# A four-layer cross-attention stack: the two batches in flight are moved half a pipeline apart, and the large cross attention is cut in three

## What is computed

```python
# per batch (8 of them): x is 256 x 128, ctx is 512 x 96, all fp32
h = x + attn(ln(x), ln(x), 16 heads of 64)          # layer 0: the large one
h = h + attn(ln(h), ctx, 16 heads of 64)            #   (its scores have 512 keys)
h = h + (lin * gelu_tanh(gate)) @ w_ff2             #   gated feed-forward, 512 wide
h = ln(softmax(ln(h W_text) . ln(ctx W_audio)) (ctx W_audio) W_out + h)   # layer 1: one head
h = ln(h); h = h + attn(h, h, 16 heads of 8)        # layer 2: self attention
h = h + attn(ln(h), ctx, 16 heads of 8)             #   cross attention
h = h + gelu(ln(h) W1) W2                           #   feed-forward
h = h + attn(rotary, l2-normalised, keys and values from ctx, 16 heads of 8)  # layer 3
```

## Time and profile before

| what | value |
|---|---|
| median of 3 runs | 2421.76 us |
| the profiled execution's own time | 2438.8 us |
| its span | 2436.9 us |
| TensorE busy | 1946.3 us (80%) |
| TensorE weight load busy | 1506.8 us (62%) |
| VectorE busy | 1490.8 us (61%) |
| ScalarE busy | 1381.5 us (57%) |
| GpSimd busy | 228.8 us (9%) |
| granted TensorE clock, mean | 0.91 |
| DMA | under 1% but for the first slice |

### The profile page before, as it was taken

One profiled execution on the slowest core, in us unless ns is written; L12 is line 12 of the kernel. 1 busy time (PEld: TensorE's weight loads), 2 busy tenths in 40 slices (PEclk: granted clock), 3 DMA queues, 4 the chain that ended last, 5 costly groups with the idle time before them and its releaser, 6 DMA issues. The chain is left out here.

```text
span 2436.9 us, 40770 instructions
## 1 busy us (share of the span) xinstructions
PE 1946.3 (80%) x13984; PEld 1506.8 (62%) x13984; DVE 1490.8 (61%) x3423; ACT 1381.5 (57%) x3690; POOL 228.8 (9%) x488
## 2 busy tenths in 40 slices
PE   1889886777789987777778998777778898867877
PEld 1777665655577765555557776555556776656654
DVE  2667557775267665677436756567644665667763
ACT  1556555766455654576645554556665555446765
POOL 0000012111100001111100000121020000011111
PEclk7999998998899998898879999889888999989998
DMA  6000000000000000000000000000000000000000
GB/s 127 6 1 1 1 1 1 1 1 1 17 1 1 1 1 1 1 1 1 1 17 1 1 1 1 1 1 1 1 8 9 1 1 1 1 1 1 1 1 5
DMA packets 24162, 13.78 MB, mean 6 GB/s; under 512 B 9264, under 2 KB 23472, under 8 KB 23952
## 3 DMA queue, kind: packets, MB, share of 16 engines
q1 hardware_dynamic: 23952, 11.05, 2.0%
HBM read 9.99 MB, written 1.05 MB: 5 GB/s over the span
## 5 line engine op out<-in xcount | busy, mean ns | idle before, releaser
L1000 ACT ACTIVATE probs<-scores,nmax 128x512 f32<-128x512 f32 (+1 forms) x1024 | 586.6, 579 | 171.4 <-DVE nmax L1407 169.7
L1407 DVE TENSOR_REDUCE nmax<-scores 128x1 f32<-128x512 f32 (+1 forms) x768 | 519.6, 684 | 127.2 <-PE scores L403 73.5
L471 PE MATMUL turned<-ident,probs 128*128 128x128 f32 x3072 | 502.8, 289 | 73.2 <-ACT probs L1000 71.1
L471 PEld LDWEIGHTS turned<-ident,probs 128*128 128x128 f32 x3072 | 383.4, 148 | 164.5 <-ACT probs L1000 119.0
L773 PE MATMUL heads_out<-probs_t,v 128*32 128x256 f32 (+1 forms) x4096 | 389.0, 421 | 8.8 <-issue 4.3
L829 ACT ACTIVATE probs_t<-turned 128x512 f32<-128x512 f32 x384 | 229.1, 597 | 102.6 <-PE turned L471 96.3
L1420 DVE COPY probs_t<-turned 128x512 f32<-128x512 f32 x384 | 261.7, 681 | 26.5 <-PE turned L471 26.1
L773 PEld LDWEIGHTS heads_out<-probs_t,v 128*32 128x32 f32 (+1 forms) x4096 | 187.8, 129 | 139.3 <-issue 58.0
L740 PE MATMUL scores<-k_t,q_mask 128*128 128x256 f32 (+1 forms) x512 | 195.3, 430 | 75.4 <-POOL q_mask L1535 37.0
L1432 DVE TENSOR_TENSOR out_t<-heads_out,scale_t 128x256 f32<-128x256 f32 x192 | 81.5, 425 | 272.2 <-ACT scale_t L829 272.2
L1535 POOL CAST q_mask<-q_t 32x256 fp32r<-32x256 f32 x384 | 156.2, 407 | 659.4 <-PE scores L740 222.9
(11 more groups left out here) (309 smaller groups left out, 3273.3 us busy)
## 6 DMA issues: line engine op xcount, KB each, us to landing
out_t<-ctx_dram SPq DMA_DIRECT2D x8, 192.0 KB, 2.6
v<-wqt_dram SPq DMA_DIRECT2D x2, 512.0 KB, 5.1
wo<-wo_dram SPq DMA_DIRECT2D x2, 512.0 KB, 6.4
x<-x_dram SPq DMA_DIRECT2D x8, 128.0 KB, 2.4
y_dram<-x SPq DMA_DIRECT2D x8, 128.0 KB, 1.8
v<-wkt_dram SPq DMA_DIRECT2D x1, 512.0 KB, 5.0
probs_t<-wv_dram SPq DMA_DIRECT2D x1, 512.0 KB, 6.6
wff<-wff_dram SPq DMA_DIRECT2D x1, 512.0 KB, 5.8
```

Source lines behind the costliest of these rows:

```text
L471: return nc.tensor.transpose(out, in_, ident[:, :])
L1000: last = nc.scalar.activation(probs[:, n % 3, k * S:k * S + ph.keys], bank[:, k * S:k * S + ph.keys], ACT.Exp, bias=nmax[:, h * QB + qb:h ...
L1407: nc.vector.tensor_reduce(out, src, AX.X, ALU.max, negate=True).then_inc(sem["attention_max"], 1)
```

## The change

The two streams run half a pipeline apart: while stream a is in layer 0 (self0 and cross0), stream b is in layers 2 and 3. cross0 is cut in three phases of 6, 6 and 4 heads (12, 12 and 8 units), and the phases of the two streams alternate. Per half round there are seven phases: self0 of a beside mid1 of b; self2 of b beside mid0 of a; cross0a beside mid2 of b; cross2 of b with no chain; cross0b beside mid3 of b; l3 of b with no chain; cross0c beside the end of b and the start of its next batch. The first segment now holds a lone start, self0, mid0 and cross0 of batch 0 (with the start of batch 1), and the last one ends with a drain: mid1, self2, mid2, cross2, mid3, l3 and end of the last batch, each alone.

The bank X is needed by layer 0 in most phases now, so the chains use it as a second bank only in mid0 and in the drain; mid2 and mid3, which had it before, have Y alone in the loop. `v1` gets its own buffer, `scale_t` has one slot in place of two, and the loads are issued between the stores.

```diff
-PAIR = [("self0", 0, [("start", 1)]), ("self0", 1, [("mid0", 0)]), ("cross0", 0, [("mid0", 1)]),
-        ("cross0", 1, [("mid1", 0)]), ("self2", 0, [("mid1", 1)]), ("self2", 1, [("mid2", 0)]),
-        ("cross2", 0, [("mid2", 1)]), ("cross2", 1, [("mid3", 0)]), ("l3", 0, [("mid3", 1)])]
+def half_round(a, b, start=True):
+
+    return [("self0", a, [("mid1", b)]), ("self2", b, [("mid0", a)]), ("cross0a", a, [("mid2", b)]),
+            ("cross2", b, []), ("cross0b", a, [("mid3", b)]), ("l3", b, []),
+            ("cross0c", a, [("end", b)] + ([("start", b)] if start else []))]
+
+
+def drain(s):
+
+    return [("", 0, [("mid1", s)]), ("self2", s, []), ("", 0, [("mid2", s)]), ("cross2", s, []),
+            ("", 0, [("mid3", s)]), ("l3", s, []), ("", 0, [("end", s)])]
 
 
 SEGMENTS = {
-    "first": [("", 0, [("start", 0)])],
-    "loop": PAIR + [("l3", 1, [("end", 0), ("start", 0)]), ("", 0, [("end", 1)])],
-    "last": PAIR + [("l3", 1, [("end", 0)]), ("", 0, [("end", 1)])],
+    "first": [("", 0, [("start", 0)]), ("self0", 0, []), ("", 0, [("mid0", 0)]),
+              ("cross0a", 0, [("start", 1)]), ("cross0b", 0, []), ("cross0c", 0, [])],
+    "loop": half_round(1, 0) + half_round(0, 1),
+    "last": half_round(1, 0, start=False) + drain(1),
 }
...
-    spare = content in ("g1", "l1", "s1", "p1", "qkv1", "up1", "kv1", "qt1", "kt1", "kt3", "t1")
-    if chain == "start":
-        spare = s == 0 and content in ("v1", "v3")
-    return "spare" if spare and (chain, s) != ("mid1", 0) else "chain"
+    if chain == "mid0":
+        spare = content in ("v1", "v3", "v5", "v7")
+    else:
+        alone = SEGMENT == ["last"] and s == 1 and chain != "start"
+        spare = alone and content in ("g1", "l1", "s1", "p1", "qkv1", "up1", "kv1", "qt1", "kt1", "kt3", "t1")
+    return "spare" if spare else "chain"
...
 PACE = {
-    ("mid0", 0): {"hat": 0.5, "v2": 4, "v4": 1.6, "v5": 1.6, "v7": 4},
...
-    ("start", 1): {"ctx": 0.8, "stats": 4, "ln1": 0.64, "split": 6.25, "v0": 1.6, "v1": 4, "v3": 2.5},
+    "mid0": {"hat": 0.5, "v2": 4, "v4": 1.6, "v5": 1.6, "v7": 4},
+    "mid1": {"l0": 0.3},
+    "mid3": {"unit": 1.6},
+    "end": {"wo": 4},
+    "start": {"ctx": 0.8, "ln1": 0.64, "split": 4, "v0": 1.6, "v1": 1.6, "v3": 2.5},
 }
...
-        scale_t = sb("scale_t", [P, 2, S])
+        scale_t = sb("scale_t", [P, S])
...
             with sp.Fori(0, LOOPS) as b:
                 enter("loop")
-                load(1, b * STREAMS + 1)
-                store(0, b * STREAMS)
-                load(0, b * STREAMS + 2)
-                store(1, b * STREAMS + 1)
+                for s in range(STREAMS):
+                    store(s, b * STREAMS + s)
+                    load_context(s, b * STREAMS + s + 2)
+                    stored(s)
+                    load_tokens(s, b * STREAMS + s + 2)
                 segment_over()
```

More of the change, by code:

```diff
@@ L84 @@
 MAKE = {"self0": lambda s: Attention("self0", s, 2, S, t_rows=D),
-        "cross0": lambda s: Attention("cross0", s, 2, T, t_rows=C),
+        "cross0a": lambda s: Attention("cross0a", s, 2, T, t_rows=C, heads=(0, 6)),
+        "cross0b": lambda s: Attention("cross0b", s, 2, T, t_rows=C, heads=(6, 12)),
+        "cross0c": lambda s: Attention("cross0c", s, 2, T, t_rows=C, heads=(12, H)),
         "self2": lambda s: Attention("self2", s, 4, S, masked=True),
@@ L138 @@
             "pads": "mid1", "squares": "mid3", "root": "mid3"}
+SEGMENT = []
 ORDER = []
@@ L166, in enter @@
 def enter(segment):
-    for table in (ORDER, PHASES, FILL, NORM, SPLIT):
+    for table in (SEGMENT, ORDER, PHASES, FILL, NORM, SPLIT):
         table.clear()
+    SEGMENT.append(segment)
     fills = {"chain": 0, "spare": 0}
@@ L195, in precedes, with groups_out @@
     return first in ORDER and ORDER.index(first) < ORDER.index(second)
+def groups_out(layer, s, chain, group):
+    for (name, ps), ph in PHASES.items():
+        at = group - ph.first // ph.group
+        if name.startswith(layer) and ps == s and 0 <= at < ph.groups and precedes((name, s), (chain, s)):
+            return ph.at("out_scaled", at + 1)
+    return 0
 def early_t(ph):
@@ L211 @@
 PACE = {
-    ("mid0", 0): {"hat": 0.5, "v2": 4, "v4": 1.6, "v5": 1.6, "v7": 4},
-    ("mid0", 1): {"hat": 0.25, "astats": 0.6, "v1": 1.6, "audio_t": 0.6, "v4": 1.6, "v5": 1.6, "v7": 8},
-    ("mid1", 0): {"l0": 0.3},
-    ("mid1", 1): {"that": 0.4, "text_t": 0.4, "p1": 0.4, "qkv1": 2.5, "qt1": 0.5, "kt0": 0.5},
-    ("mid2", 1): {"stats": 0.3},
-    ("mid3", 0): {"unit": 1.6},
-    ("mid3", 1): {"unit": 1.6},
-    ("start", 1): {"ctx": 0.8, "stats": 4, "ln1": 0.64, "split": 6.25, "v0": 1.6, "v1": 4, "v3": 2.5},
+    "mid0": {"hat": 0.5, "v2": 4, "v4": 1.6, "v5": 1.6, "v7": 4},
[3 more added lines that the diff above has]
+    "start": {"ctx": 0.8, "ln1": 0.64, "split": 4, "v0": 1.6, "v1": 1.6, "v3": 2.5},
 }
 def due(steps, units):
-    pace = [PACE.get((name, s), {}).get(step, 1.0) for name, s, step in steps]
+    pace = [PACE.get(name, {}).get(step, 1.0) for name, s, step in steps]
     return {step: int(sum(pace[:n]) * units / sum(pace)) for n, step in enumerate(steps)}
@@ L718, in queries_times_m @@
                     pe.wait_ge(sem["attention_t_lo"], ph.at("t_lo", h))
-                three_products(X[0:ph.t_rows, 0:S], (m_hi[layer][:, h, :], m_lo[layer][:, h, :]),
+                if h == 0 and ph.spare_fills:
+                    pe.wait_ge(sem["spare_bank_read"], ph.spare_fills)
+                m = ph.first + h
+                three_products(X[0:ph.t_rows, 0:S], (m_hi[layer][:, m, :], m_lo[layer][:, m, :]),
                                (x_hi[ph.s][:, :], x_lo[ph.s][:, :])).then_inc(sem["attention_t"], 1)
@@ L782, in attention @@
             def attention(ph):
-                chain, contents = {"self0": ("start", ("v2", "v3")), "cross0": ("mid0", ("v7",)),
+                chain, contents = {"self0": ("start", ("v2", "v3")), "cross0a": ("mid0", ("v6", "v7")),
+                                   "cross0b": ("mid0", ()), "cross0c": ("mid0", ()),
                                    "self2": ("mid1", ("kt0", "kt1")), "cross2": ("mid2", ("kt2", "kt3")),
@@ L1431, in scale_out @@
                 dve.wait_ge(sem["attention_scale"], ph.at("scale", g + 1))
-                nc.vector.tensor_tensor(out_t[ph.s][:, g, :], O[:, 0:S], scale_t[:, g % 2, :], ALU.mult
+                nc.vector.tensor_tensor(out_t[ph.s][:, ph.first // ph.group + g, :], O[:, 0:S], scale_t[:, :], ALU.mult
                                         ).then_inc(sem["attention_out_scaled"], 1)
```

59 lines of the change are left out of this document (35 added, 24 removed).

## The result

The changed kernel takes 2806.07 us, median of 4 runs (2795.58 to 2813.72), beside 2423.26 us for the kernel before. The ratio is 1.1565, with a 95% interval of 1.1528 to 1.1602. Slower was forecast, but the time lies outside the range of 2450 to 2770.

A forecast was written before the change was run, and what follows sets the result against it. No engine was full; the chains' latency on strictly in-order engines was taken to bound the kernel. Fill and drain 445 + 7 x 314 = 2643, with 27 for the clock 2670, lowered to a forecast of 2650 us; range 2450 to 2770.

The forecast's parts named there:

- the start of the first half round: End of the fill, after batch 0 runs its first phases: first full half round forecast to start at 222 us.
- P and C: Estimated lengths for each pairing: P, the phase without a chain; C, the chain without a phase.
- What a pairing costs: Each phase-chain pairing costs its longer part plus 0.35 of the smaller; 0.15 and 0.6 kept as ends.
- Two lengths: Step estimating lone phase and chain lengths from interleaved rows; phases sum to 207.5 us per batch.
- The 58 (62 with the refill): mid1 with one bank: fills at 1.24 us, statistics, splits, exponentials and stacks; 4 us more refills the attention pipeline.
- With a second bank some 5 less: mid1's chain would be some 5 us shorter if it had two banks.
- gains most: self2 with mid0, forecast at 40 us: mid0 leaves PE-bound phases, so this pairing was to gain most.
- The 27 us for fill and drain: Clock term: lone chains' PE work of about 55 us runs at a lower clock, between 8 and 55 us more.
- Only fill and drain are lost: Rival: a half round costs what a batch does now, 298.6 us; total 2562, in runs 2547; chance 0.25.
- The interleaving works: Rival: the change is faster, deciding from a share of 0.10; 2390 us at 0.05; chance 0.12.
- The chains block layer 0: Rival: PE queues each mid1 and mid3 step behind a unit; half round 348 us, time 2893; chance 0.15.

The follow-up runs named there:

- run 9: Changed kernel with each phase and each chain of the half rounds run alone, banks as in that kernel: 3211.85 us (ratio 1.3228).
- Run 1: Changed kernel with mid1 run alone ahead of self0 instead of between its units: 2926.92 us (ratio 1.205).
- run 4: Changed kernel with cross0 cut into 4, 8 and 4 heads instead of 6, 6 and 4: 2855.68 us (ratio 1.1764).
- run 2: Kernel before with the chains' second bank taken away except for start, order unchanged: 2521.84 us (ratio 1.0389).
- run 7: Changed kernel with bank X shared in time between layer 0's products and the chains' fills: 2680.22 us (ratio 1.099).
- runs 5 and 6: Each chain step issued ahead of its attention unit: changed kernel 2806.83 us (ratio 1.1546), kernel before 2496.61 us (1.0264).

## Why the prediction was right in direction and wrong in size

**Right.** What the forecast called the reason held: cross2 and l3, 64 of the 128 units, stand without a chain, and what they could hide is lost. cross2 alone (43.5 forecast, 44.1), l3 alone (26, 24.3), cross0b with mid3 (56, 58.1) and the start of the first half round (222, 216.8) came within 7%. The sum of all lone lengths was right too: its P and C sum to 402 per half round, and the trace with everything alone gives 401.1. That is in part luck: mid1 was too short by nearly what the phases were too long.

**The steps that failed.** The main one is in "What a pairing costs": that 0.35 of the smaller part stays in view and the rest is hidden. By it the half round hides 402 - 314 = 88 us. Measured are 59.1. As the sum of the lengths was right to 0.9 us, this is the miss of 28. The 0.35 was even below the mean of its own rows, 0.39.

The other is a length in "Two lengths", mid1 with one bank. The 58 (62 with the refill) was counted from fills at 1.24 us each, a price read between attention units, where four turns kept PE 0.60 us. In the lone chain (run 9) four turns take 1.11 us, and two fills stand 1.8 to 1.9 us apart; with two banks 0.9:

```profile
677.86 1.11 PE L496 MATMUL chain_bank<-ident,out_t 128*128 128x128 f32 x4 [0.69 <-ACT q_t L858]
679.75 1.12 PE L496 MATMUL chain_bank<-ident,v 128*128 128x128 f32 x4 [0.78 <-DVE q_t L1188]
3044.74 1.11 PE L496 MATMUL chain_bank<-ident,out_t 128*128 128x128 f32 x4 [2.99 <-DVE v L1180]
3045.65 1.06 PE L496 MATMUL queries_m<-ident,out_t 128*128 128x128 f32 x4
```

25 fills at some 0.6 more would be 15 us (an estimate from these rows), and mid1 took 72.9 for 58. With two banks the forecast had 53, and 53.6 and 56.8 were measured. So "With a second bank some 5 less" is mis-sized: it is 16 to 19 less.

The lone lengths by pairing follow. Here the phase is the stretch from its first exponential on ScalarE to its last, and the chain with its handover is the time from there to the next phase's first:

| pairing | phase + chain, forecast | phase + chain, alone | together | hidden |
|---|---|---|---|---|
| self0, mid1 | 42 + 62 | 34.7 + 75.7 | 91.6 | 18.8 |
| self2, mid0 | 32 + 24 | 23.0 + 28.5 | 45.9 | 5.6 |
| cross0a, mid2 | 26 + 27 | 19.4 + 31.7 | 39.3 | 11.8 |
| cross0b, mid3 | 26 + 47 | 20.5 + 50.7 | 58.1 | 13.1 |
| cross0c, end and start | 17 + 29.5 | 12.8 + 36.5 | 38.6 | 10.7 |

(75.7 is 72.4 for mid1 and 3.3 of handover behind self0. The border between start and mid1, which follow each other there, is set by choice, so that the 72.4 are what mid1 adds to the half round. Run 1 gives 72.8 for that: from cross0c's first exponential to self0's it takes 111.4 us on average with a lone mid1 between them, and 38.6 in the change. The rest, cross2 and l3, is 43.9 and 23.7 alone and hides nothing.)

The first two columns don't count alike: a handover of 3 to 5 us is in the chain when alone, and the forecast has it in the phase. With it moved, mid0, mid2 and mid3 come out at some 24, 27 and 47, as forecast. Wrong are self0 and self2, 38 and 27 where 42 and 32 were taken, end and start, some 3 too short, and mid1, 10 too short. The half round is then 273 + 128 x share, an estimate from the same rows. At 0.35 that is 318, so the wrong lengths cost 4 of the 28 us, mid1's 10 being mostly given back by phases that were taken too long; the other 24 are the share, which has to be 0.54. self2 with mid0, the pairing that "gains most" in the forecast, hid the least.

Did the share hold across the change? With the lone lengths of before (the smaller of the two sums to 153 per batch, of which 79.2 is hidden) it is 1 - 79.2/153 = 0.48. In the changed kernel the smaller ones sum to 110.4 and 59.1 is hidden: 0.46. So counted, the share of the whole held, and by it a half round is 401.1 - 0.52 x 110.4 = 344, where 342.0 was measured. But with the handovers moved to the phases the smaller parts are some 152 and 128, the shares 0.48 and 0.54, and the half round by the share of before is 335. So the two kernels don't show that the share is a constant. This was worked out after the result, and run 4 speaks against using it phase by phase: there 28.0 us of cross0b beside mid3 hid 14.0, little more than the 13.1 that 20.5 hid.

**Where the 23 us of longer lone work come from**, per batch, from the same two traces: mid1 +7.9 (75.7 against the mean of 77.7 and 57.9), mid2 +7.5, mid3 +9.1, end and start +4.1, handovers behind phases that now have no chain +7.1; mid0 with two banks -9.2, the exponentials' stretches -3.1. Part of mid1, mid2 and mid3 is the lost bank, shown by run 2, by run 7 with the reserve stated there, and for mid1 by the lone lengths. That mid2 and mid3 also differ because another phase stands ahead of them is argued from the table alone.

**Clock.** The 27 us for fill and drain did not appear: the drain took 215.4 where 236 was forecast without them. The clock did fall in it (0.83; 0.74 in its lone mid1). I read this as a price that the lengths held already, since they were taken from stretches whose clock was low as well; no run separates it. The Trainium skill (TensorE: Matmul & The Clock Gate, HAM oscillation) has PE drop to half rate when its idle gaps are long; the forecast took from it that the short gaps inside a lone chain would not cost the clock. The lone mid1 with one bank does not agree with that reading. Its granted clock is 0.57, so PE was at the lower of its two levels, 1.2 GHz, for most of it. Its gaps on PE are about 1 us in the rows of run 9, and elsewhere up to 3.0 us, with one of 7.4 us at 660.0. The clock was down before that one: from 638.3 to 660.0 it is 0.50.

```profile
638.30:660.00 21.70, 11.55 (x30) 7.29 (x30) 5.90 (x17) 3.10 (x7) 0.69 (x1) 0.50 0.00 1
667.43 0.69 PE L496 MATMUL chain_bank<-ident,xhat 128*128 128x128 f32 x2 [7.41 <-DVE xhat L1141]
```

**The rivals.** "Only fill and drain are lost" (298.6 per half round) fell: seven half rounds cost 2370 - 7 x 298.6 = 280 us more than seven batches before, and all that lies outside them 2802.4 - 2370 = 432 beside 2436.9 - 7 x 298.6 = 347, 85 more. "The interleaving works" fell: no half round is under 336. "The chains block layer 0" had the size, 348 per half round, and its sign, self0 with mid1 over 85 us, was there. mid1 takes 82 to 88 us between self0's units and 72.9 alone, so steps do queue; a step put one unit earlier won nothing in runs 5 and 6, and no run took the queueing away. The Trainium skill (Perfetto Trace Analysis, Optimization Strategy) says that performance may be improved by such a mixing of regimes; here it was not, with a ratio of 1.1565.

**Open.** With the bank shared (run 7) the two middle half rounds fall by 17 us on average, from 343.7 to 326.8; the 28 us that are left above 298.6 were not undone one by one. How the 20 us less that is hidden divide into queueing and phases without a chain was not measured. Why self2 hides only 5.6 us of mid0, and why the chain put first costs 2.6% before and nothing after, was not tried.

## What to carry to other kernels

Before moving chains of dependent steps between phases, measure each phase and each chain alone in one run with nothing beside anything: their sum and how much is hidden now would have come within 7 us of the half round here (335 or 344 for 342.0), where the estimates from interleaved stretches missed by 28. Count then what the smaller part of each new pairing is; a phase left without a chain hides nothing, and a longer phase beside the same chain need not hide more of it. A second buffer in a latency-bound chain is worth more than its fills suggest, since each step both waits for its reader and leaves the engine idle, at a lower clock.

## What the runs showed that was not expected

- The same products keep PE busy for 484.7 us per pair before (clock 0.91), 527.7 in the changed kernel (264.06 + 263.63, 0.88) and 566.8 with everything alone (283.48 + 283.33, 0.78).
- The loss of a second bank goes with a lower granted clock: 0.57 against 0.66 in the lone mid1 of the changed kernel, 0.56 against 0.75 in that of the kernel before, where PE's busy time goes from 28.08 to 37.30 us for the same 130 matmul records.
- mid3 hid 12.5 to 14.5 us in the four pairings that were tried: 12.5 in cross2 (39.5 + 42.8 - 69.8) and 14.5 in l3 (20.8 + 40.5 - 46.8) before, 13.1 and 14.0 in cross0b with 12 and with 16 units.
